# Where a banded attention kernel puts the mask of its scores into PSUM: a ScalarE copy in the place of an identity product on TensorE

## The reference, cut to what matters

```
q, k, v = split(shift_tokens(x) @ Wqkv)
q = l2norm(q) * q_scale;  k = l2norm(k) * k_scale;  rotary(q), rotary(k)
mask = (it < jb) | (it > jb + 32) | (jb == -1)        # a band over the own and the previous window
sim  = where(mask, -max, q @ k2.T * 8)
x = softmax(sim) @ v2 @ Wo + x
x = (a * gelu(gate)) @ W2 + b2 + x                    # a, gate from the LayerNorm of shift_tokens(x)
```

## Time and profile before

| | us |
|---|---|
| median of 3 runs | 3797.96 (3797.13 to 3800.81) |
| the profiled execution | 3794.33 |
| its span, first to last instruction | 3792.6 |
| TensorE (PE) busy | 3308.5 (87%) |
| VectorE (DVE) busy | 2844.1 (75%) |
| ScalarE (ACT) busy | 2302.5 (61%) |
| GpSimd (POOL) busy | 2253.0 (59%) |
| mean granted TensorE clock | 0.958 of full |

### The profile page before, as it was taken

The page is one execution under the profiler, slowest core; times in us unless marked ns, Lnnn a source line. Parts: engine busy times, 40 slices in busy tenths (PEclk is TensorE's granted clock), DMA queues, the critical chain, the costliest instruction groups (busy, mean ns, idle before and its releaser), DMA issues. The chain is left out here.

```text
span 3792.6 us, 150168 instructions
## 1 busy us (share of the span) xinstructions
PE 3308.5 (87%) x64584; PEld 2479.7 (65%) x64970; DVE 2844.1 (75%) x3988; ACT 2302.5 (61%) x4617; POOL 2253.0 (59%) x1982
## 2 busy tenths in 40 slices
PE   7848899888899889899889889889889988999985
PEld 3736666666666666666666666666667666666663
DVE  5348778777777787877877877878777787777783
ACT  4326666666656666666666666666666666666664
POOL 0037666666666666666666666666666666666661
PEclk9769999999999999999999999999999999999998
DMA  1021011011111011111101101101101011110112
GB/s 30 20 71 37 28 31 31 28 29 59 31 29 31 28 29 59 31 29 31 31 27 59 32 28 31 29 29 60 31 28 31 29 31 56 30 32 28 30 30 71
DMA packets 94827, 133.97 MB, mean 35 GB/s; under 512 B 21065, under 2 KB 45152, under 8 KB 93280
## 3 DMA queue, kind: packets, MB, share of 16 engines
q1 hardware_dynamic: 86508, 123.78, 11.0%
q10 hardware_dynamic: 7668, 0.50, 0.2%
HBM read 25.60 MB, written 4.26 MB: 8 GB/s over the span
## 5 line engine op out<-in xcount | busy, mean ns | idle before, releaser
L1022 POOL TENSOR_TENSOR qs<-rprod 128x512 f32<-128x512 f32 x768 | 993.6, 1303 | 843.2 <-DVE rprod L1092 827.8
L1092 DVE TENSOR_TENSOR rprod<-ps,tab 128x1024 f32<-128x1024 f32 x768 | 923.0, 1219 | 402.9 <-PE ps L779 315.6
L1033 POOL TENSOR_TENSOR qs<-qs,rr 128x512 f32<-128x512 f32 x768 | 805.7, 1070 | 276.7 <-ACT rr L964 276.7
L777 PE MATMUL ps<-wh,xls 128*128 128x512 f32 x1152 | 587.2, 510 | 50.8 <-PEq L733 39.7
L828 PE MATMUL ps<-pt,v 64*64 64x32 f32 x24768 | 443.6, 221 | 184.6 <-ACT pt L954 181.7
L828 PEld LDWEIGHTS ps<-pt,v 64*64 64x64 f32 x24768 | 400.1, 135 | 262.8 <-ACT pt L954 227.9
L788 PE MATMUL ps<-con,qs 128*128 128x128 f32 x3080 | 513.6, 290 | 0.0
L942 ACT ACTIVATE sq<-ps 128x512 f32<-128x512 f32 x384 | 228.4, 595 | 441.7 <-PE ps L779 437.7
L1038 POOL TENSOR_TENSOR pr<-pr,rinv 128x512 f32<-128x512 f32 x386 | 403.1, 1044 | 124.8 <-DVE rinv L1134 124.2
L807 PE MATMUL ps<-kT,qT 64*32 64x64 f32 x24704 | 423.7, 218 | 57.5 <-DVE gx L1140 0.8
L1110 DVE TENSOR_REDUCE ssq<-sq 128x16 f32<-128x1024 f32 x384 | 464.0, 1208 | 0.0
(11 more groups left out here) (159 smaller groups left out, 5005.2 us busy)
## 6 DMA issues: line engine op xcount, KB each, us to landing
v<-v SPq DMA_DIRECT2D x384, 192.0 KB
v<-v SPq DMA_DIRECT2D x288, 64.0 KB
raw<-in_L_ffn_Wqkv SPq DMA_DIRECT2D x7, 1536.0 KB, 7.4
wo<-in_L_ffn_Wo SPq DMA_DIRECT2D x6, 512.0 KB, 8.8
sT<-so SPq DMA_DIRECT2D x22, 96.0 KB, 1.6
bias<-in_L_attn_hidden_states SPq DMA_DIRECT2D x8, 256.0 KB, 5.6
srow<-sT SPq DMA_DIRECT2D x8, 256.0 KB, 3.3
xrow<-in_L_attn_hidden_states SPq DMA_DIRECT2D x8, 256.0 KB, 4.0
```

What stands on the lines that cost most here:

```text
L777: nc.tensor.matmul(dst, al, bh, start=True, stop=False)
L1022: nc.gpsimd.tensor_tensor(qs[:, i % 2, j].rearrange("p (h s d) -> p h s d", s=2, d=HALF), prod[:, 0, j].rearrange("p (h s d) -> p h s d", ...
L1033: nc.gpsimd.tensor_tensor(q3, q3, rr[:, 8 * j:8 * j + 8].unsqueeze(2).broadcast_to([P, 8, DH]), ALU.mult).then_inc(cur["mul"], 1)
L1092: return nc.vector.tensor_tensor(prod[:, :, j, :].rearrange("p c (h d) -> p c h d", d=DH), ps[:, bank, :].rearrange("p (h d) -> p h d", d= ...
```

## The change

In the full rounds the mask product leaves TensorE. ScalarE copies the mask (`maskb`, bf16) into bank SC of PSUM, float32, and TensorE's scores, which have `start=False` as before, accumulate onto it. A new semaphore `mk` tells TensorE that the mask is there; the waits for `sub`, `gl` and `h` move from TensorE to the ScalarE copy. The copy for slot i + 1 stands at the end of slot i for i from 1 to 6, behind kT and ahead of that slot's extra; the copy for slot 0 stands at the head of slot 0, behind the table load of slot 7; the copy for slot 1 stands inside slot 1, between the square of q and the copy of v. One mask product at the head of the block, with `start=True`, leaves the bank in the state in which later matmuls accumulate. The two drain rounds keep the mask product.

```diff
--- before.py
+++ after.py
@@ -188,7 +188,7 @@
 
 ROUND = ("aq ak v tq tk S tp o sqk sqq vev pte qte ln r exp ote kte rq rk ss g m sub rs ri add mul prm "
          "woa wo mean var gup aup w2 xh xl fq fr fh gl h x2 x1 fx fc fn fl "
-         "wh wl w1h w1l vc tab shifted cleared").split()
+         "wh wl w1h w1l vc tab mk shifted cleared").split()
 
 
 def chunked_attention(nc, t, ctx, sb0, sem0, clear, con, ident, ps, xT, sT):
@@ -790,13 +790,16 @@
 
             def scores(i):
                 hf, tb = unit(i, 2)
-                after(pe, "sub", i)
-                if i == 0 and pb0 is not None:
-                    pe.wait_ge(other["gl"], 3)
-                if i == 1 and pb0 is not None:
-                    pe.wait_ge(cur["h"], 3)
-                nc.tensor.matmul(ps[:, SC, :], identb[:], maskb[:, int(tb > 0), :], start=True, stop=False,
-                                 skip_group_check=True)
+                if full:
+                    pe.wait_ge(cur["mk"], i + 1)
+                else:
+                    after(pe, "sub", i)
+                    if i == 0 and pb0 is not None:
+                        pe.wait_ge(other["gl"], 3)
+                    if i == 1 and pb0 is not None:
+                        pe.wait_ge(cur["h"], 3)
+                    nc.tensor.matmul(ps[:, SC, :], identb[:], maskb[:, int(tb > 0), :], start=True, stop=False,
+                                     skip_group_check=True)
                 after(pe, "qte", i)
                 after(pe, "kte", i)
                 for hp in range(4):
@@ -933,15 +936,28 @@
                 act.wait_ge(cur["sub"], i + 1)
                 nc.scalar.activation(pr[:, i % 2, :], pr[:, i % 2, :], ACT.Exp).then_inc(cur["exp"], 1)
 
+            def write_mask(i, st):
+                nc.scalar.copy(ps[:, SC, :], maskb[:, int(unit(i, 2)[1] > 0), :]).then_inc(st["mk"], 1)
+
             for i in range(only):
                 hf0, tb0 = unit(i, 1)
                 hf3, tb3 = unit(i, 3)
+                if full and i == 0:
+                    after(act, "sub", 0)
+                    if pb0 is not None:
+                        act.wait_ge(other["gl"], 3)
+                    write_mask(0, cur)
                 if full:
                     act.wait_ge(cur["ak"], i + 1)
                     after(act, "ss", i)
                     nc.scalar.activation(sq[:, 1, :], ps[:, BB, :], ACT.Square).then_inc(cur["sqk"], 1)
                     act.wait_ge(cur["rq"], i + 1)
                     nc.scalar.activation(sq[:, 0, :], ps[:, A, :], ACT.Square).then_inc(cur["sqq"], 1)
+                    if i == 1:
+                        if pb0 is not None:
+                            act.wait_ge(cur["h"], 3)
+                        act.wait_ge(cur["sub"], 1)
+                        write_mask(1, cur)
                     act.wait_ge(cur["v"], i + 1)
                     nc.scalar.copy(v[:, 0, i % TB, (i // TB) * S:(i // TB + 1) * S], ps[:, O0, :]) \
                         .then_inc(cur["vev"], 1)
@@ -978,6 +994,9 @@
                     act.wait_ge(cur["tk"], i + 1)
                     nc.scalar.copy(kT[:, hf0, :, WIN + tb0 * P:WIN + tb0 * P + P],
                                    ps[:, T0, :].rearrange("p (a n) -> p a n", a=4)).then_inc(cur["kte"], 1)
+                if full and 1 <= i < 7:
+                    act.wait_ge(cur["sub"], i + 1)
+                    write_mask(i + 1, cur)
                 if i == 3 and nb is not None:
                     shift_high(nb, 1 - k).then_inc(cur["xh"], 1)
                 if new_hf0 and 4 <= i < 7:
@@ -1193,11 +1212,14 @@
     with nc.Block(no_gpsimd_drain=True) as block:
         @block.tensor
         def _(pe):
+            nc.tensor.matmul(ps[:, SC, :], identb[:], maskb[:, 0, :], start=True, stop=True,
+                             skip_group_check=True).then_inc(s_hi, 1)
             program(pe, lambda r: r["tensor"])
 
         @block.scalar
         def _(act):
             nc.scalar.preload_act_table_set(LN_EXP)
+            act.wait_ge(s_hi, 4)
             program(act, lambda r: r["scalar"])
 
         @block.gpsimd
```

## The result

| | before | after |
|---|---|---|
| median, us | 3799.4 | 3899.5 |
| ratio of the runs, 95% interval | | 1.026 (1.024 to 1.028) |
| the profiled execution, us | 3794.33 | 3903.02 |
| span, us | 3792.6 | 3901.2 |
| PE busy, us | 3308.5 | 3354.5 |

The change makes the kernel 100 us slower. 3872 was forecast with a range from 3810 to 3928.

A forecast was written before the change was run, and what follows sets the result against it. TensorE was taken to bound slots 1 to 4, VectorE 5 and 6, a VectorE-ScalarE chain 7 and 0. 47 rounds at +1.30 us (+61) plus 13 for the clock on 3794.3 gave 3868, as median 3872 us; range 3810 to 3928.

The forecast's parts named there:

- The product's price: Mask product on TensorE: worth 0.21 us each (low bound 0.15) where TensorE runs without a gap, slots 1 to 4.
- The copy: Mask copy on ScalarE: 0.53 us of the engine (bounds 0.48 and 0.63), 0.60 us until it has landed.
- Slot 0: Copy between table load and square of k, no idle time on ScalarE: TensorE ends the slot at +0.53 us.
- Slot 1: Copy behind the square of q: scores get a new wait of 0.9 us, the slot costs +0.70 us.
- Slots 2 and 3: Copy hidden in ScalarE's idle time at the slot's end: TensorE gains 0.21 us in each, -0.42 us.
- Slots 4 and 5: Slot 4: late square of k delays the second rotary product, net +0.19 us; slot 5: 0, copy fits idle time.
- slack ahead of `x1`: Slot 4, VectorE: 0.22 us to spare ahead of `x1`, taken off its +1.22 us shift to leave +1.00.
- Slot 7: Copy ahead of `fr` delays the square of k: +0.53 us in one round read, +0.08 in another, mean +0.30.
- The clock: More TensorE idle time, 0.7 us more a round at half clock, 0.39 us per us: +13 us, bounds 0 and +60.
- The clock rival: One more half-clock stretch in each round, +61 us in the place of +13: 3920 us, chance 15%.
- The faster rival: TensorE limits every slot it fills and copies hide; slots 1 to 4 gain 0.21 us each: 3759 us, chance 8%.
- The partly hidden rival: Half-clock rounds give ScalarE idle time in slots 7 and 0; only slots 1 to 4 count: 3820 us, chance 13%.

The follow-up runs named there:

- the kernel with `xhs` moved: Kernel before, with ScalarE mask copies for slots 2, 3 and 4 only and the `xhs` instructions moved from slot 3's end to slot 2's: 3792.3 against 3802.6 us, 0.9977.

## Why the prediction was right, and what it mis-sized

The direction, the mechanism and the range held. Point by point:

- **The product's price**, 0.21 us in a gapless slot: 0.17 to 0.21 measured, and 0.22 where it was added. That slots 5 to 7 pay nothing held too (products issued twice there: 1.0010). That TensorE's saving in slot 4 goes into a wait held as well: the kernel with `xhs` moved gets nothing for it.
- **The copy**: 0.60 us long as forecast, 0.51 to 0.53 us of the engine in the timelines above, inside the bounds. The Trainium skill's note that ScalarE writes PSUM faster than SBUF (ScalarE: Activation LUTs, "Step-by-step: what each stage is for") agrees in the duration, 0.60 against 0.63 us for `fq`, but brought nothing to the sum: the low bound of 0.48 us was not reached.
- **Slot 0**: +0.53 forecast, +0.52 at full clock, and the kernel with this copy alone has the same 10.17 us.
- **Slot 1**: +0.70 forecast, +0.74. The wait of 0.9 us ahead of the scores is there as 0.88.
- **Slots 2 and 3**: -0.42 forecast, -0.38.
- **Slots 4 and 5, the term that failed**: +0.19 forecast, +0.43. Up to the square of k the walk is right: it stood 1.99 us into the slot and stands at 2.42, +0.43, for which the prediction has 1.22 - 0.81 = +0.41. Then it took off 0.22 us of slack ahead of `x1`, and `x1` does begin only 0.15 us later. But the slack isn't worth anything. GpSimd's product hangs on `rinv`, ahead of that slack, and the copy of `fx`, which the prediction left at its 0.46 us, ended 0.28 us behind GpSimd's product in 41 of 48 rounds before and in 36 after. Slots 4 and 5 together change as the start of that product does, in three kernels: -0.01 against 0.00 us with the `xhs` instructions moved, +0.21 against +0.21 with slot 4's copy alone, +0.43 against +0.44 with the whole change. 0.24 x 47 = 11 us of the error.
- **Slot 7**: +0.30 forecast as a mean of +0.53 and +0.08, +0.47 measured over all rounds. The two rounds that were read are not half and half: before the change ScalarE was idle ahead of that square of k (over 0.05 us) in 18 of 48 rounds, after it in 3. 0.17 x 47 = 8 us.
- **The clock**: the +13 us came out near the 20 measured by luck, as two errors cancel. The rounds got 133 us more at half clock, 2.8 us each, where 0.7 were assumed; and such a us cost about 20 / 133 = 0.15 us (an estimate, all that isn't at full clock put down to the clock), where 0.39 was taken, read from two whole rounds, one at full clock and one not.

The clock rival, at 3920 us, asked for one more half-clock stretch in each round, 3.4 us. With 2.8 us its condition nearly came true, and 3899.5 lies nearer to it than to the forecast; its price did not, since 20 us and not 61 go with the clock.

The faster rival, at 3759 us, needed the copies of slots 0 and 1 to hide. Slot 0 alone costs 37 us and slot 1 alone 58, so it falls by its own condition. The partly hidden rival at 3820 us falls too: slots 0 and 7 cost +0.70 and +0.47 us in the mean of all rounds.

What stays open: why a kernel whose slots 2 and 3 are shorter (copies there alone) gets its half-clock stretches so often at the end of slot 7 and ends level with the one before. Single copies add up to 37 + 58 + 2 + 14 + 17 = 128 us, and together they cost 100 (slots 5 and 6 were not tried alone). At full clock the rounds of the single ones add up to +1.5 us, less than the +1.84 of the whole change, so what they have too much lies in their half-clock rounds. The runs show that time and clock go together, and what a stretch costs in which place, not what sets the place.

## What to carry to other kernels

Moving work from a nearly full engine to one at 61% paid here only where the first had no wait, the second had idle time right there, and no third engine was the limit. Walk it place by place: three of eight products had cost nothing and a fourth was worth nothing when it went; the copies for slots 2 and 3 fell into idle time, and those for slots 0, 1, 4 and 7 stood on a chain. A copy that a consumer must wait for belongs ahead of that consumer by its full length, 0.6 us here. When you count slack, ask who branches off ahead of it: GpSimd did here. And the best gain lay beside the change, in taking two small copies, 1.1 us together in that kernel, off the engine that limits two slots.

## What the runs showed of the hardware that was not expected

- The duration of a VectorE copy from SBUF to SBUF (64x512, float32) depends on GpSimd. It ended 0.28 us behind the end of GpSimd's product in 41 of 48 rounds before and 36 after, and took 0.46 or 0.75 us in the two rounds above according to how early it began; with no such product beside it it took 0.42. Its mean is 0.525 us in the kernel before, 0.683 in the changed one and 0.710 with slot 4's copy alone. The Trainium skill, SBUF — State Buffer, "SBUF: two separate sides", says that VectorE's two-port operations and GpSimd share a port pair under an exclusive lock and the loser is blocked until the other has ended; the durations agree with that, and no run here takes GpSimd's product away to prove it.
- More work on TensorE made the kernel faster: 12 products a round in its idle time brought the mean clock of the runs to between 0.972 and 0.977, where it was between 0.951 and 0.959, and took off 20 us (0.9954).
- What half clock costs depends on where it falls. Slot 7 lasts 11.62 us without it, mostly less with a stretch about its start, and 13.4 us with one that begins 8 us or more into it.
- TensorE accumulated onto what ScalarE had written into PSUM in all 384 places, after one product with `start=True` at the head of the block and the feed-forward products in the same bank. No run leaves that product out.
